# A macaron of attention and expert layers: new engine orders for 25 slots, a fifth place for expert weights, and full attention's scores over 128 rows beside zeros

## The reference: what is computed

```python
# layer 1, "ffn": causal attention, 16 heads of 8; layer 2, attention in blocks; layer 3, full attention
scores = jnp.einsum('bhsd,bhed->bhse', q, k) * scale        # 512 x 512 a head and sequence
attn = jax.nn.softmax(scores, axis=-1)
out = jnp.einsum('bhse,bhed->bhsd', attn, v)

# layer 2, "ffn": every token goes to the expert of its largest gate
for i in range(E):                                          # E = 8
    h = jnp.einsum('bsd,df->bsf', x, w1[i]) + b1[i]         # 128 -> 1024
    a, g = jnp.split(h, 2, axis=-1)
    y = jnp.einsum('bsh,hd->bsd', a * jax.nn.sigmoid(g), w2[i]) + b2[i]
    out = out + jnp.where((top1 == i)[..., None], y, 0.0)
```

## Time and profile before

| | |
|---|---|
| median of 3 runs | 3220.77 us (3209.05 to 3223.18) |
| the profiled execution | 3222.13 us, span 3220.3 us |
| mean granted TensorE clock | 0.894 |
| TensorE busy (matmul) | 2716.4 us, 84% |
| TensorE weight loads | 1722.2 us, 53% |
| VectorE busy | 2240.2 us, 70% |
| ScalarE busy | 1693.2 us, 53% |
| GpSimd busy | 848.8 us, 26% |
| chain that ended last | TensorE 49%, VectorE 23%, ScalarE 8%, issue 5% |

### The profile page before, as it was taken

The page is one execution under the profiler, slowest core; times in us unless marked ns, Lnnn a source line. Parts: engine busy times, 40 slices in busy tenths (PEclk is TensorE's granted clock), DMA queues, the critical chain, the costliest instruction groups (busy, mean ns, idle before and its releaser), DMA issues.

```text
span 3220.3 us, 64240 instructions
## 1 busy us (share of the span) xinstructions
PE 2716.4 (84%) x24502; PEld 1722.2 (53%) x24561; DVE 2240.2 (70%) x5340; ACT 1693.2 (53%) x4134; POOL 848.8 (26%) x875
## 2 busy tenths in 40 slices
PE   5857788898886789998777888899998888999996
PEld 2545455544444444467755777556563332465664
DVE  4656567788876668864466545887887677788783
ACT  2235443565622365542357434676765666776772
POOL 1010001122111222112233124555541112555550
PEclk8767777899977799998899999999998888999997
DMA  2524410000000000036510366100100000101010
GB/s 104 219 38 66 65 51 1 1 1 1 1 1 1 1 1 1 1 125 247 188 54 2 122 229 202 42 21 21 26 16 3 1 1 1 24 16 26 16 33 10
DMA packets 136844, 159.38 MB, mean 49 GB/s; under 512 B 84949, under 2 KB 111829, under 8 KB 135002
## 3 DMA queue, kind: packets, MB, share of 16 engines
q1 hardware_dynamic: 134010, 150.09, 15.7%
q0 software_dynamic: 2048, 4.20, 0.4%
q10 hardware_dynamic: 480, 0.98, 0.1%
HBM read 106.53 MB, written 30.61 MB: 43 GB/s over the span
## 4 chain that ended last, share of the span: by engine, by line
PE 49%; DVE 23%; ACT 8%; issue 5%; POOL 4%; DMA 3%; SPq 2%; POOLq 0%; DVEq 0%; ACTq 0%
DVE nm L1181 5%; PE ps L1915 4%; PE ps L1140 4%; PE ps L529 3%; PE ps L2117 3%; PE ps L1117 3%; PE ps L1081 3%; PE ps L2283 3%; ACT hand L494 2%; PE ps L387 2%; DMA hand<-in_experts 2%; PE ps L602 2%; PE ps L266 2%; PE ps L2420 2%; PE ps L1900 1%
## 5 line engine op out<-in xcount | busy, mean ns | idle before, releaser
L1181 DVE TENSOR_REDUCE nm<-ps 128x2 f32<-128x256 f32 (+2 forms) x704 | 428.5, 644 | 104.3 <-PE ps L1081 50.2
L1230 ACT ACTIVATE core<-ps 128x512 f32<-128x512 f32 x672 | 360.8, 588 | 100.4 <-PE ps L1122 61.4
L2189 POOL TENSOR_TENSOR pre<-pre,sin 128x512 f32<-128x512 f32 x128 | 236.9, 1871 | 251.7 <-ACT pre L2160 211.0
L328 POOL TENSOR_TENSOR rstd<-ve,weights 128x4 f32<-128x4 f32 x80 | 81.0, 1013 | 843.1 <-DVE ve L305 839.2
L1081 PE MATMUL ps<-hand 128*128 128x128 bf16 (+4 forms) x993 | 239.4, 319 | 46.9 <-DVE nm L1181 42.1
L494 ACT COPY hand<-ps 64x512 bf16<-64x512 bf16 x320 | 185.5, 580 | 152.0 <-PE ps L529 95.3
L1117 PE MATMUL ps<-hand 128*128 128x128 bf16 (+4 forms) x996 | 213.4, 305 | 9.6 <-ACT hand L494 5.4
L1915 PE MATMUL ps<-hand 128*128 128x128 f32 x1408 | 197.4, 300 | 25.5 <-DMA hand<-in_experts 25.4
L2194 POOL TENSOR_TENSOR ss<-ss,weights 128x16 f32<-128x16 f32 x64 | 199.2, 3112 | 72.9 <-DVE ss L2209 71.1
L2323 ACT ACTIVATE core<-ps,nm 128x128 f32<-128x128 f32 x512 | 182.1, 376 | 64.8 <-DVE nm L2340 64.3
L1915 PEld LDWEIGHTS ps<-hand 128*128 128x128 f32 x1408 | 188.1, 215 | 35.3 <-DMA hand<-in_experts 29.3
(11 more groups left out here) (339 smaller groups left out, 6663.9 us busy)
## 6 DMA issues: line engine op xcount, KB each, us to landing
hand<-in_experts SPq DMA_DIRECT2D x88, 836.0 KB, 8.0
shear<-post SPq DMA_DIRECT2D x64, 256.0 KB
core<-shear SPq DMA_DIRECT2D x256, 32.0 KB, 1.9
hand<-hand SPq DMA_DIRECT2D x16, 512.0 KB, 4.4
hand<-hand SPq DMA_DIRECT2D x16, 384.0 KB, 5.6
pre<-sorted_in SPq DMA_DIRECT2D x8, 704.0 KB, 4.9
sorted_out<-core SPq DMA_DIRECT2D x88, 64.0 KB
core<-in_stream SPq DMA_DIRECT2D x2, 2048.0 KB, 8.4
```

Source lines behind the costliest of these rows:

```text
L1181: nc.vector.tensor_reduce(nm_of(unit), src, AX.X, ALU.max, negate=True).then_inc(negmax, 1)
L1230: nc.scalar.activation(prob8[:, i % PROBS, 0:w], m.ps[:, RING[at % NR], 0:w], ACT.Exp).then_inc(ring_out, 1)
L2189: ins = nc.gpsimd.tensor_tensor(o[:, :, :, z:z + hl], x[:, :, :, y0:y0 + hl], sn[:, t, :, z:z + hl].unsqueeze(2).to_broadcast([P, 2, LH, h ...
```

## The change

Five edits:

1. `PLACES` is 5. The fifth place is in the core's own buffer (columns 3584 to 5256, which the experts' core leaves free); tile i uses place i % 5.
2. Layer 3's full attention uses `score_rows` as the others do: q in `QX` beside zeros, scores over 128 rows; its pre clears q on GpSimd and copies each turned pair in three pieces (L494 twice, L541) in place of one (L538), and `take_q` copies each turned q in two (L494) in place of one (L1207).
3. `turn_stacks` gets `on_vector`, the pairs that VectorE copies. It is empty for the pre of layer 1's second causal attention on sequences 2 and 3 (slots 21 and 22), where ScalarE copies all eight; elsewhere it is as before.
4. The orders of slots 20 to 39 and 43 to 47 are others. Of their strings one for SyncE stands below, for an experts' slot (a the core, b the pre with its read of the sorted rows).
5. Some strings of the table are only broken into lines in another way.

```diff
-PLACES = 4
+PLACES = 5
...
-def turn_stacks(nc, m, lane, a, stkk, ready, cleared=None, once=False):
+def turn_stacks(nc, m, lane, a, stkk, ready, cleared=None, once=False, on_vector=(1, 3, 5, 7)):
...
     def scalar(act):
-        for pair in range(0, 8, 2):
-            yield 2.0 * pair + 0.8
-            take(act, nc.scalar.copy, pair)
+        for pair in range(8):
+            if pair not in on_vector:
+                yield 2.0 * pair + 0.8
+                take(act, nc.scalar.copy, pair)
 
     def vector(dve):
-        for pair in range(1, 8, 2):
+        for pair in on_vector:
...
-                q, k = (half_rows if kind == FULL else score_rows)(a, h)
+                q, k = score_rows(a, h)
...
-            if kind != FULL:
-                copy_q(nc.scalar.copy, a, 2 * g + n, m.psb[:, RING[at % NR], 0:L]).then_inc(ring_out, 1)
-            else:
-                nc.scalar.copy(a.QK[:, 2 * g + n, 0:L], m.psb[:, RING[at % NR], 0:L]).then_inc(ring_out, 1)
+            copy_q(nc.scalar.copy, a, 2 * g + n, m.psb[:, RING[at % NR], 0:L]).then_inc(ring_out, 1)
...
-    turn_stacks(nc, m, lane, a, s.stkk, stacked, cleared)
+    turn_stacks(nc, m, lane, a, s.stkk, stacked, cleared, on_vector=() if l == 1 and b >= 2 else (1, 3, 5, 7))
...
-    return rope_attn_pre(nc, m, lane, a, b, m.weight["l3a_qkv"], "l3a_qkv_b", True, True)
+    return rope_attn_pre(nc, m, lane, a, b, m.weight["l3a_qkv"], "l3a_qkv_b", True, False)
...
-     "sync": "a8b1a4"},
+     "sync": "a7b1a5"},
...
-        ("l1_ffn", l1_ffn_pre, l1_ffn_core, l1_ffn_post, 0),
+        ("l1_ffn", l1_ffn_pre, l1_ffn_core, l1_ffn_post, 1),
...
-        m.ring = [hands[1].whole[:, i * EXPERT:(i + 1) * EXPERT] for i in range(PLACES)]
+        m.ring = [hands[1].whole[:, i * EXPERT:(i + 1) * EXPERT] for i in range(PLACES - 1)]
...
-            a.xs = a.whole[:, PLACES * EXPERT:PLACES * EXPERT + TILES * P]
+            a.xs = a.whole[:, (PLACES - 1) * EXPERT:(PLACES - 1) * EXPERT + TILES * P]
...
         m.core = sb("core", 5632)
+        m.ring.append(m.core[:, 3584:3584 + EXPERT])
```

More of the change, by code:

```diff
@@ L557, in turn_stacks @@
     lane.pairs = pairs
-    lane.add(17.0, tensor=tensor, scalar=scalar, vector=vector)
+    if on_vector:
+        lane.add(17.0, tensor=tensor, scalar=scalar, vector=vector)
+    else:
+        lane.add(17.0, tensor=tensor, scalar=scalar)
     return lane.taken, f + 8
@@ L2613 @@
[L2613 to L2620 removed]
+    {"tensor": "b2a6b1a14b1a1b1a1b1",
+     "vector": "b4a1b1a1b6a2b3a1b1a1c1a6",
+     "scalar": "b1a2b1a9b3",
+     "gpsimd": "e1b1c1b1",
+     "sync": "a8b1a2d1a2"},
+    {"tensor": "b2a7b1a14b1a1b2",
+     "vector": "b7a2c1b3a1b1a1b3a1b1a7",
+     "scalar": "b2a11b3",
```

241 lines of the change are left out of this document (117 added, 124 removed).

## The result

Twenty runs of each kernel: before 3216.3 us median, after 3207.4. One of the twenty of the change was a slow run, 3594.6 us at a mean granted clock of 0.67, which the ratio leaves out; the others took 3187.7 to 3214.0. The ratio is 0.9969, 95% interval 0.9955 to 0.9983: 10 us faster, within half a per cent. The forecast was 35 us, so its size was wrong; the time lies inside the range.

What follows compares the result with a forecast made beforehand. No single engine bounds the kernel throughout; layer 3's full attention, slots 44 to 47, ran at a mean clock of 0.88. Terms -18 + 8 + 3 - 16 - 4 - 8 = -35 us, from 3222.1 to 3187 us; range 3145 to 3228.

Steps and rivals of the forecast that it cites:

- The lead: Slots 44 to 47, 22 first scores running ahead: 128 rows keep the clock up, -18 us, between 0 and -21.
- The new order helps by itself: Start of slots 44 to 47: 17 first scores in a row (8 before in slot 45), projections later; some 6 us.
- The lost overlap: Layer 3, slots 44 to 47: 128-row scores can no longer run in pairs, +8 us, between 0 and +28.
- Copies: Layer 3's full attention: more copies of turned q and layout, mostly covered by ScalarE's idle time, +3 us, 0 to +18.
- All q copies on the path: Layer 3, slots 44 to 47: upper end for added copies, none of the turned q's copying hidden, +18 us.
- Nothing: Layer 3: GpSimd's clearing of q, 3.5 us a unit, runs while GpSimd is little busy and costs no time.
- The fifth place: Experts, slots 24 to 27 and 32 to 35: loads issued sooner cut TensorE's 25.3 us wait, -16 us, 0 to -25.
- Slots 21 and 22: Layer 1's second causal attention: four of eight pairs go from VectorE to ScalarE, -4 us, between 0 and -10.
- Other orders: Slots 20 to 39 and 43: same work reordered, sorted rows read earlier, -8 us, between +15 and -25.
- overlap lost and copies decide: Rival, slots 44 to 47: TensorE takes 28 us and ScalarE 18 on the path, 3243 us, slower; chance 0.13.
- the clock's rival: Slots 44 to 47: the clock stays low despite 128 rows, only order gains some 6 us, 3199 us; chance 0.17.
- orders pay everywhere: Rival, all 25 slots: reordering closes idle time, terms at their good ends, 3141 to about 3150 us; chance 0.13.

Runs made afterwards that it cites:

- rows alone: Before with layer 3's full-attention scores over all 128 rows, both heads summed, no zeros, copies or clearing: slots 44 to 47 27.3 us less, ratio 0.9947; new orders 0.9897.

## Why the prediction was right and wrong

1. **The lead** (-18). The mechanism was right: rows raise the clock with either order, and alone they give 17.5 us. In the change the lead gave 8.2 (22nd maximum at 19.4, 17.8, 19.9 and 19.3 us). "The new order helps by itself" was wrong: with 64 rows it moves the four 22nd maxima by 0.3 us in all, and with the rows alone it puts 7.8 us back ahead of them. It helps where the clearing waits: 85.1 us for the four maxima with 128 rows and copies in the old orders, 76.4 in the change.
2. **The lost overlap** (+8). Wrong in sign. I priced what 64 rows gain and not what they cost at each change to 128-row work, nor that the clock also falls after the lead: rows alone took 9.9 us off there. These two are some 10 and 6 us by estimate against 23.5 for the pairs, so they don't explain the sign by themselves; what covers the rest is open. The upper end, +28, was far off.
3. **Copies** (+3): the step that failed. I compared ScalarE's idle time, 65 us, with 29.7 us of new work and called it covered. Alone, they cost 15.3 and 17.4 us. My reading, which the runs price but don't prove, is that the idle time of an engine that empties a three-bank ring is the ring's waiting, and a longer copy lengthens every turn of it. "All q copies on the path" was my upper end, 18, and should have been the value; the layout's copies, 11.6 us on ScalarE and 9.2 on VectorE, had no bound of their own beyond that. GpSimd's clearing, "Nothing", was nothing only because the new order moved VectorE's step: in the old order VectorE waited 8.3 us in slots 45 and 46 each, and moving the step took 7.6 us off.
4. **The fifth place** (-16): right in size. 18 us by the means with the new orders of slots 24 to 35, 13 of them in slots 24 to 27, though the waits were larger in slots 32 to 35; 12 by the place alone, and by the ratio 14 (0.9955).
5. **Slots 21 and 22** (-4): wrong sign in these slots, +4.5 to +7, and no gain in the whole (0.9996). "TensorE is the busier engine" was the hint that moving work between the other two gains nothing; I read it as a small gain all the same. Which wait makes slot 21 longer was not tried further.
6. **Other orders** (-8): -2 in slots 20 and 23, 28 to 31 and 36 to 39 within what executions differ by, +2 to +4 in slots 40 to 43 (1.5 of it in slot 43, by the copies of the first layout). About zero.

Where the 35 us went, by the slots of the two profiles, which differ by 16 us where the ratio says 10: layer 3 gave 3 for 7 forecast, slots 21 and 22 lost 4.5 for 4 gained, the other orders gave nothing for 8, and the fifth place came as forecast. That layer 3 missed by only 4 us is luck: the copies cost 26 us more than I had, and the rows gave back more than I had after the lead, where I expected a loss.

The change in layer 3, summed in the old orders: rows -27.3, copies +15.3 and +14.1, waiting for the clearing 7.6, makes +10 against 11.7 measured. The new orders turn this into -3. Beyond the 7.6 us for the clearing, why they gain with copies and lose without stays open, and with one profile of each kernel part of it may be the execution.

Of the rivals, "overlap lost and copies decide" had the right half: the copies. Its overlap half, the clock's rival and "orders pay everywhere" fell. The chances gave 0.20 to no change, and that is what came.

## What to carry to other kernels

Idle time on an engine inside a short ring is no cover: cost added work there at its full price until a run shows less. When a layout change raises TensorE's utilisation, try it first with the arithmetic changed and no extra copies; that one run gives the ceiling (27 us in the slots here, 17 in the whole), and the copies can be priced against it. A step that waits for another stream's buffer blocks its in-order queue, so look at what stands behind it, and an order tuned for one version is no gain by itself for another.

## What the runs showed of the hardware

- The granted clock followed the rows in use, with the same instructions, counts and orders: 0.88 with 64-row scores, 1.00 with 128 (78.5 us at half clock and none). The Trainium skill (TensorE: Matmul & The Clock Gate, "What's actually happening") speaks of how busy the array is; here the number of rows counted too.
- A score behind a score with other rows starts 0.32 us after it, behind one with the same rows 0.22 (512 columns, full clock).
- Added waiting came with a lower clock: 18 to 21 us of added copies went with 17 to 20 us more at half clock. The price of half clock in this kernel, from two times of the same code, is 6.7 us for 17.1.
- The same code before slot 20 took 1084 to 1109 us in different executions, and slots 44 to 47 either 325 or 332. A gain under half a per cent needs runs of the whole and several profiles, not one pair.
